# Differential attention: the value matmuls cut into steps of 256 queries and spread between the scores

## The reference

```python
qs = (x @ Wq.T).reshape(b, s, H, 2, F)
ks_ = (x @ Wk.T).reshape(b, s, H, 2, F)
vs = (x @ Wv.T).reshape(b, s, H, DH)
scores = jnp.einsum('bqhif,bkhif->ibhqk', qs, ks_) * scale
atts = jax.nn.softmax(scores, axis=-1)
att = atts[0] - diff_weight * atts[1]
o = jnp.einsum('bhqk,bkhe->bqhe', att, vs)
```

## Time and profile before

| | us |
|---|---|
| median of 3 runs | 2037.39 |
| lowest and highest | 2030.86, 2041.65 |
| the profiled execution's own time | 2050.52 |
| its span | 2048.7 |
| stage of kind 2, first to last item | about 1031 to 1398 |
| stage of kind 3, first to last item | about 1745 to 1935 |
| TensorE busy in the span | 1591.5 (78%) |
| VectorE, ScalarE, GpSimd busy | 1125.9, 876.7, 405.2 |

### The profile page before, as it was taken

One profiled execution on the slowest core, in us unless ns is written; L12 is line 12 of the kernel. 1 busy time (PEld: TensorE's weight loads), 2 busy tenths in 40 slices (PEclk: granted clock), 3 DMA queues, 4 the chain that ended last, 5 costly groups with the idle time before them and its releaser, 6 DMA issues. The chain is left out here.

```text
span 2048.7 us, 27214 instructions
## 1 busy us (share of the span) xinstructions
PE 1591.5 (78%) x9284; PEld 901.3 (44%) x9284; DVE 1125.9 (55%) x2483; ACT 876.7 (43%) x1919; POOL 405.2 (20%) x520
## 2 busy tenths in 40 slices
PE   4799565699999857487389999995585676999668
PEld 3577455255555456386122222223574442222245
DVE  5345643133333442511788888875413676788556
ACT  2211223444444324121178888783121234777522
POOL 0444044000000035176130000000275001000000
PEclk7899677799999969598599999997698786999869
DMA  1000155312020046277520202000386014221000
GB/s 64 0 1 0 46 167 172 102 22 62 2 61 1 7 148 210 88 253 203 145 68 6 72 1 73 1 1 10 114 271 175 16 50 129 71 64 26 1 0 20
DMA packets 90367, 149.84 MB, mean 73 GB/s; under 512 B 13441, under 2 KB 64513, under 8 KB 89601
## 3 DMA queue, kind: packets, MB, share of 16 engines
q1 hardware_dynamic: 80576, 129.08, 21.2%
q0 software_dynamic: 7936, 16.27, 3.0%
q10 hardware_dynamic: 1728, 2.88, 0.7%
HBM read 111.49 MB, written 36.70 MB: 72 GB/s over the span
## 5 line engine op out<-in xcount | busy, mean ns | idle before, releaser
L1737 DVE TENSOR_REDUCE MAXI<-psum 128x2 f32<-128x1024 f32 x384 | 457.4, 1220 | 91.3 <-PE psum L1563 88.5
L1662 ACT ACTIVATE EX<-psum 128x512 f32<-128x512 f32 x768 | 413.0, 606 | 105.0 <-PE psum L1584 104.9
L1584 PE MATMUL psum<-QM,KM 64*128 64x512 bf16 x768 | 227.9, 385 | 28.2 <-ACT EX L1662 21.4
L2000 PE MATMUL psum<-EX,N 128*128 128x512 f32 x512 | 239.1, 610 | 0.0
L2051 ACT ACTIVATE EX<-psum 128x512 f32<-128x512 f32 x256 | 149.1, 598 | 177.8 <-PE psum L1992 177.8
L1563 PE MATMUL psum<-KM,QS 64*128 64x512 bf16 x768 | 185.6, 403 | 35.9 <-DVE MAXI L1737 15.5
L1594 PE MATMUL psum<-EX,VST 128*32 128x512 f32 x1536 | 203.2, 604 | 1.0 <-ACT OT L1676 1.0
L906 POOL DMA_INDIRECT m_XG<-rows,m_ROWS x124 | 121.7, 982 | 404.1 <-DVE m_ROWS L1103 367.5
L249 PE MATMUL psum<-ident,N 128*128 128x128 f32 x192 | 50.1, 433 | 160.6 <-DVE N L229 160.6
L944 PE MATMUL psum<-m_XT,m_W 128*128 128x128 f32 x992 | 146.5, 295 | 33.7 <-DVE m_XT L1123 20.1
L1130 DVE TENSOR_SCALAR m_Y<-psum 128x128 f32<-128x128 f32 x124 | 36.2, 292 | 228.6 <-DMA y<-m_Y,m_ROWS 148.0
(11 more groups left out here) (285 smaller groups left out, 2300.0 us busy)
## 6 DMA issues: line engine op xcount, KB each, us to landing
m_W<-in_w_dram SPq DMA_DIRECT2D x124, 512.0 KB, 5.0
parts<-PART SPq DMA_DIRECT2D x36, 256.0 KB, 2.2
parts<-PART SPq DMA_DIRECT2D x12, 384.0 KB, 2.5
parts<-PART SPq DMA_DIRECT2D x36, 128.0 KB, 2.1
rows<-N SPq DMA_DIRECT2D x4, 1024.0 KB, 5.1
N<-y SPq DMA_DIRECT2D x16, 256.0 KB, 4.2
parts<-FIX SPq DMA_DIRECT2D x16, 256.0 KB, 2.9
QS<-parts SPq DMA_DIRECT2D x32, 128.0 KB, 3.9
```

Source lines behind the costliest of these rows:

```text
L1584: pe.matmul(bank_of(("score", n, i)), KM[r, buf, g, m, kt * P:(kt + 1) * P], QM[r, n % 2, MAPS[at] // slots, :], start=True, stop=True).th ...
L1662: act.activation(EX[:, n % 2, kt, MAPS[j], :], bank_of(("score", n, i)), ACT.Exp, scale=SM_SCALE).then_inc(S["exp"].sem, 1)
L1737: dve.tensor_reduce(MAXI[:, n % 2, qt, columns], pair(i), AX, ALU.max, negate=True).then_inc(S["reduced"].sem, 1)
L2000: last = pe.matmul(banks[4 + j], N[:, n // per_b * TB + kt, :], EX[:, n % 2, kt, j, :], start=kt == 0, stop=kt == TB - 1)
```

## The change

The first value step of an item stays whole (128 keys, 512 queries). Each of the other three is cut into two halves of 256 queries, so an item has seven steps. Their places become after the scores 1, 4, 7, 9, 11, 13 and 15. The places move from after scores 11 and 13 to after 10 and 12, on TensorE, in the ring and on ScalarE (the shifts). The take (after exp 0), the gather (after score 6), the keep and the projections stay.

```diff
-        AT_PLACE = (11, 13)[:stacks]
-        AT_VALUE = (4, 8, 12, 15)
+        AT_PLACE = (10, 12)[:stacks]
+        AT_VALUE = (1, 4, 7, 9, 11, 13, 15)
+        VALUES = ((0, 0, L),) + tuple((c, half * L // 2, (half + 1) * L // 2) for c in range(1, TB) for half in range(2))
...
-                def value(n, c):
+                def value(n, step):
+                    c, at, to = VALUES[step]
                     pe.wait_ge(S["exp"].sem, at16("exp", n, 4 * c + 3))
                     if c == 0:
                         pe.wait_ge(S["vstage"].sem, S["vstage"].at(n + 1))
                         if n and n % GROUP == 0:
                             pe.wait_ge(S["taken"].sem, S["taken"].at(n // GROUP))
                     for j in range(4):
-                        last = pe.matmul(banks[4][32 * j:32 * j + 32, :], VST[:, n % 2, c, j // 2, :],
-                                         EX[:, n % 2, c, j, :], start=c == 0 and n % GROUP == 0,
-                                         stop=c == TB - 1 and ended(n) is not None)
-                    if c == TB - 1:
+                        last = pe.matmul(banks[4][32 * j:32 * j + 32, at:to], VST[:, n % 2, c, j // 2, :],
+                                         EX[:, n % 2, c, j, at:to], start=c == 0 and n % GROUP == 0,
+                                         stop=step == len(VALUES) - 1 and ended(n) is not None)
+                    if step == len(VALUES) - 1:
                         last.then_inc(S["value"].sem, 1)
...
-                for c in range(TB):
-                    value(items - 1, c)
+                for step in range(len(VALUES)):
+                    value(items - 1, step)
```

## The result

The changed kernel takes 2063.84 us (median of 4 runs, 2057.13 to 2066.11) against 2039.52 for the kernel before, ratio **1.012** (95% interval 1.008 to 1.016): +24 us, 17 to 33. Run again later, beside e9 and e10, it gave 1.011 (1.007 to 1.015). It is slower, by more than the 15 us forecast and inside the stated range.

The account below looks back on a forecast made before the run. TensorE was taken as the bound. Kind 2 (3 - 0.6) and kind 3 (11 + 1.4, for waiting on the take, cut values and places) summed to +15 us on the 2037.39 median: 2052 us, range 2031 to 2074.

Parts of the forecast that it names:

- The half at 0.57 and the entry at 0.23: On TensorE between scores, a half value step holds it 0.57 us; each visit to the values pays 0.23 us entry.
- The wait for the take: TensorE's first value step, now after score 1, waits 1.4 us for the take that ScalarE runs after exp 0.
- The items: Item lengths: kind 3 from 12.38 to 13.40 us; kind 2 with take 11.73 to 12.54, without 10.61 to 10.0.
- 0.7 of cut values: TensorE's value steps per item go from 4.4 to 5.05 us by cutting, 0.7 more, from three more entries.
- About 0.2 for places: In kind 3 items, places that now begin and end away from a wait add about 0.2 us on TensorE.
- The sum: Whole program, both changed stages: kind 2 and kind 3 effects together add 15 us.
- the sum for kind 2: Kind 2 stage: 15 pairs at +0.2 us make 3, less 0.6 for the first item with values.
- two of the eleven also project; I add 0.7 each: Two kind 3 items with projections, where waits for REST hide some of a value step: 0.7 us more each, 1.4 together.
- the clock at 1.00: Whole changed kernel: the granted clock stays at 1.00, the full 2.4 GHz, listed as a sign of being right.
- Rival 1: Value step 0 finds the take done, so the 1.4 us wait goes: about -24 us, 2014, faster; chance 0.10.
- Rival 2: ScalarE and VectorE catch up in the waiting, halves' entries cost under 0.23: +4 us, 2041, no change; chance 0.28.
- rival 3: Halves cost by instruction, each holding TensorE 1.04 us, not 0.57: +130 us, 2180; chance 0.04.

Follow-up runs that it names:

- e9: The changed kernel with the places back after scores 11 and 13, cut and value spots kept; ratio 1.005 to the kernel before.
- e10: The changed kernel with the take ahead of exp 0, first value step after score 2, places back after 11 and 13; ratio 0.985 to the kernel before.
- e2: Halves as in the change, but together in the four old spots (after scores 4, 8, 12, 15), places after 11 and 13; ratio 0.999 to the kernel before.
- e1: The changed kernel with the take ahead of exp 0 instead of behind it, on ScalarE alone; ratio 0.996 to the kernel before.
- e4: The kernel before with four whole value steps after scores 1, 7, 11, 15 and places after 10 and 12; ratio 1.027 to the kernel before.
- e11: The changed kernel as it is, run again on the same chip as two other versions; ratio 1.011 to the kernel before.
- e5: The changed kernel with the take ahead of exp 0 and the first value step after score 2 in place of 1; ratio 0.988 to the kernel before.
- e7: The kernel before with only the take moved ahead of exp 0; ratio 0.993 to the kernel before.

## Why the prediction was right, and where it was off

- **The half at 0.57 and the entry at 0.23** held: 0.57 in the rows, and the run of 56 value matmuls at the stage's end lasts 3.66 us, as the 32 of the earlier trace rows did (3.64). The Trainium skill's rule ("TensorEngine Tiling (Array Packing)", Key Properties), that a change of tiling mode drains TensorE, agrees: the same halves cost nothing in four visits (e2), and each change of tile shape that the rows show costs about 0.09, from a score to a value step, from a score to a place and from a place to a half.
- **The wait for the take** held: 1.32 us of recorded idle time, 30 times with the one at the end, 39.2 us in all, and e1 shows that in plain items it is paid in full.
- **The items** held: 13.34, 12.48 and 9.98 against 13.40, 12.54 and 10.0.
- **The ledger of "0.7 of cut values"** was right as TensorE time and wrong as a cause. In the old spots, the halves together, the cut costs nothing (e2); in the new ones it is worth 0.65 (kind 3) and 1.9 (a pair of kind 2) against the four whole steps of e4.
- **"About 0.2 for places"** was half of it: e9 shows 0.43 in kind 3. The sum still came out, since the chain by items had the lost pairs in it.
- **The sum** of the two stages was 15 us and they measured 17, partly by luck: kind 3 was put 1.3 us too high and kind 2 3.5 too low.
- **The term that was mis-sized is the sum for kind 2**: 2.4 us forecast, 5.9 measured; kind 3 had 12.4 and 11.1. Plain pairs rose by 0.12 (I had 0.2), the missing part is in the three pairs with a projection, which I had at nothing extra: 24.99, 25.68, 25.68 us became 26.20, 28.83, 27.35, +6.0. The step "two of the eleven also project; I add 0.7 each" was applied to kind 3 only (where it was 0.3: those items went from 16.10 to 17.36). In kind 2 TensorE waits there for VectorE's REST, the subtraction that reads a projection's bank and so frees it for a score. Before and after, in the same item of the second sequence, and after in that of the third:

```profile
1147.61 0.39 PE L1584 MATMUL psum<-QM,KM 64*128 64x512 bf16 x2 [0.87 <-DVE REST L1728]
...
1139.63 0.61 PE L1585 MATMUL psum<-QM,KM 64*128 64x512 bf16 x2 [1.34 <-DVE REST L1730]
1140.17 2.08 PE L1547 MATMUL psum<-nT,WQK 128*128 128x512 f32 x2
...
1235.83 0.39 PE L1585 MATMUL psum<-QM,KM 64*128 64x512 bf16 x2 [1.34 <-DVE REST L1730]
1236.15 1.13 PE L1547 MATMUL psum<-nT,WQK 128*128 128x512 f32 x2
```

- Each of these items has two such waits; they grew from 0.87 and 0.25 to 1.34 and 0.88, 1.1 us of the 1.5 that the pair of the third sequence gained beyond a plain pair. VectorE is busy without a pause for 11.31 us before the first of them (1128.27 to 1139.58): reductions, the mixing work and REST follow each other. So here VectorE holds TensorE up, where the prediction had TensorE as the bound.
- In the first of the two items the granted clock falls as well: the stretch 1139.60 to 1143.00 in the part on the result stands at 0.52, so mostly at 1.2 GHz, and the projection takes 2.08 us (1.13 at 2.4 GHz). The item of the next sequence, with the same wait, stays at 2.4 GHz and is 1.5 us shorter (14.89 against 16.38 from copy to copy); e11 has the long one again (16.43). The prediction had the clock at 1.00 throughout.
- **The rest**: stages give 17 us, the median 24 (interval 17 to 33). Whether the other 7 are there is open. The rest of the program, outside the stages, went from 1503 to 1493 us in the two profiles of before and after, the other way; but the profiled execution before (2050.5) was slower than every timed run of it. In the three profiles of e9 to e11 the rest came to 1536 to 1544 us, so one profile can't tell.
- Rival 1, the faster case, named the point that decides: the take ends before TensorE needs the bank. It did not in this kernel; in e5 and e10 it does, and they are faster by 1.2 and 1.5%. Its forecast of 12.0 for kind 3 fits e5's 11.97, though e5 also has the value step one score later. Rival 2 asked for halves under 0.66 with their entry, rival 3 for 1.04 without: they are 0.57 + 0.09.

## What to carry to other kernels

When a piece of work is moved earlier, write down for each semaphore that it waits on when that comes in the new place; here one copy of 0.6 us moved ahead of one exponential, with the step one score later, made the difference between this loss of 1.2% and e5's gain of 1.2%. Try such a move on the old kernel too: two lines moved gave 0.7% there (e7), without any cut. Small pieces spread between the scores can be worth their entry cost where TensorE would wait at that spot anyway (e4, e10 beside e7). Count the changes between kinds of work that an order makes, about 0.09 us each here, and don't break pairs that run together (0.22). Judge a spread by items with everything in them, projections too, where another engine can be the bound.

## What was not expected of the hardware

- Four matmuls on different 32-column strips with 256 columns of moving data start 0.215 us after the four before them, half of the 0.43 for 512, with no fixed part to be seen (3.66 against 3.64 us for the whole run).
- Each change among the three tile shapes costs the same 0.09 to 0.10 us over streaming: a score before a value step or a place is held 0.31 in place of 0.22, a half starts 0.15 after the last matmul of a place in place of 0.056, and a peak 0.31 after the last matmul of a half in place of 0.215. So the 0.23 of a visit is mostly two changes; the rest is that the four matmuls of a round start some 7 ns apart, and the second round of a half 0.24 after the first.
- In the first of two items with a projection a wait of 1.34 us of TensorE came just before a fall of the granted clock to half (at 1139.63, and again in e11). The same wait in the same item one sequence later, with TensorE busy 1.26 of the 2.80 us before its end (1.06 of 2.60 in the first), left the clock at 1.00, and so did the 1.32 us of waiting for the take in plain items. So the wait by itself doesn't bring the fall; what does is open.
